# W1's rows of one four-layer residual kernel: moved by on-chip transfers and turned on VectorE instead of TensorE

## Chip, cores and metric

One core of one Trainium2 chip. The metric is the device time of one execution in microseconds, lower is better.

## The reference

`x` has 8 batches of 256 rows and 1024 columns in fp32. Four layers follow each other, each `x = x + f(x)`, with weights of 1024 x 1024:

```python
x = x + (x @ W0.T + (x @ A0[lab0]) @ B0.T * 0.5)
x = x + x @ w_eff.T        # w_eff from W1, see below
x = x + (x @ W2.T + (x @ A2[lab2]) @ B2.T * 0.5)
x = x + (x @ W3.T + 2 * mixture of 8 experts, the two best of each row)
```

The second layer's weight is made from W1 with a change of low rank and a codebook of 8 levels, with one scale per group of 128 columns:

```python
lora_delta = lora_B @ lora_A * 0.5              # rank 64
normalized = (W1 + lora_delta) / scale
quantized = cb[searchsorted(thresholds, normalized)]
w_eff = quantized * scale + lora_delta
```

So `lora_delta` is added twice: before the quantising (the first of the two additions) and after it.

## The kernel before, in words

The layers are linear up to the experts, so the kernel first multiplies the weights with each other (each with the identity added, for the residual) and only then works on `x`. fp32 operands are split into a high and a low part (`_hi` by a cast on ScalarE, `_lo` by a subtraction on VectorE), and each product is three matmuls on TensorE.

The stretch that matters here runs from about 30 to 237 us of the span. TensorE runs passes 1 to 16 (`one_pass`, L1718 for their matmuls). Passes 1 to 8 multiply W2's column blocks with the turned W3 (stage 0; pass 7 is a small one for B2), passes 9 to 16 multiply the blocks of W1 with the result of that and W0 (stage 1). A pass goes over eight tiles k. In stage 1 the right side of tile k is W0's row block k with B0's columns, loaded into `w0_raw`, and the left side is one block of W1, turned, split into `w_hi` and `w_lo` (two buffers each).

W1 comes in eight row blocks of 128 rows, called n or x. For each:

1. SyncE loads it into `a_t` (L456).
2. TensorE multiplies the low-rank factors (`delta`, L1815), and ScalarE copies the result to `ldelta` (`copy_delta`, L732; two buffers).
3. VectorE adds `ldelta` (`add_delta`, L1255), GpSimd adds the identity into `ldelta` (`eye_delta`, L581), ScalarE scales each group (`normalise`, L739).
4. VectorE quantises in three parts (`quantise`, L1241 to L1246: seven thresholds, each but the first a TENSOR_SCALAR into `qtmp` and an addition into `q`), and adds `ldelta` again (L1250), which raises `w1e_done`.
5. TensorE turns the eight tiles of 128 x 128 into PSUM (`turn_w1`, L1706 with `ident,a_t`), in the middle of a pass.
6. ScalarE casts them to `w_hi` (`w1_high`, L690), VectorE subtracts to `w_lo` (`w1_low`, L1131).

Every engine executes its own list in the order written by hand in the kernel, and waits at semaphores. In VectorE's list the parts of `quantise` stand between the low parts of W2 (`w2_low`), W1 and W0 (`w0_low`, L1270). GpSimd's list in this stretch has the identity for W2 (`eye_w2`, L560), for `ldelta`, and for W0 (`eye_w0`, L586). SyncE issues all transfers: after the loads of W1 and W2 come A2's (L501), then, for k from 0 to 7, W0's and B0's row block k (L504, L505), each when TensorE has used tile k of pass 8 (`wait_used`), since `w0_raw` lies where the old low parts lay. W0's row block k then goes through GpSimd (identity), ScalarE (high part, L774) and VectorE (low part) to tile k of pass 9.

`x` is already loaded and turned later in the same way as the change does with W1: four transfers place quarters of it (L510), and VectorE turns blocks of 32 x 32 (`turn_block`, L1424), two instructions of 128 x 512 for 128 rows.

Of the kernel before, what the change touches and what calls it, by code (L numbers as in the profile page):

```python
# [53 lines left out]
def build(nc, x, lab0, codebook, lab2, lab7, W0, A0, B0, W1, scale_log, A1, B1, W2, A2, B2, W3, Wr, A3, B3, out):  # L54
# [19 lines left out]
    Q = 32  # L74
    QUARTERS = P // Q

# [76 lines left out]
    with ExitStack() as ctx:  # L153
# [46 lines left out]
        a2_raw = place("a2_raw", 154368, [P, KT, LABELS * R])  # L200
# [158 lines left out]
        n_ready = sem("n_ready")  # L359
        w1e_done = sem("w1e_done")  # L360
        w1_t = sem("w1_t")
# [87 lines left out]
        def _(sp):  # L449
# [108 lines left out]
        def _(pool):  # L558
# [19 lines left out]
            def eye_delta(n):  # L578
                pool.wait_ge(v_ready, n + 1)
                at = ldelta[n % 2][:, n * P:(n + 1) * P]  # L580
                pool.tensor_tensor(at, at, ident[:], ALU.add).then_inc(ld_eye, 1)  # L581

            def eye_w0(k):
                pool.wait_ge(w0_in[k], 32)
                at = w0_raw[:, k, k * P:(k + 1) * P]
                pool.tensor_tensor(at, at, ident[:], ALU.add).then_inc(w0_eye, 1)  # L586
# [98 lines left out]
        def _(act):  # L685
# [134 lines left out]
            w1_high(4)  # L820
            out_a(3)
            normalise(7)
# [302 lines left out]
        def _(dve):  # L1125
# [110 lines left out]
            def quantise(x, part, steps_=None):  # L1236

                n = a_t[:, x, 0:D].rearrange("p (k i) -> p k i", k=KT)
                if part == 0:
                    dve.wait_ge(n_ready, G1 * (x + 1))  # L1240
                    link(dve.tensor_scalar(q[:], n, th(0), steps[:, 0:1], ALU.is_gt, ALU.mult))  # L1241
# [3 lines left out]
                if part == 2:  # L1245
                    link(dve.scalar_tensor_tensor(out=n, in0=q[:], scalar=book[:, 0:1],  # L1246
                                                  in1=scale[:, x, :].unsqueeze(2).to_broadcast([P, KT, P]),
                                                  op0=ALU.add, op1=ALU.mult))
# [3 lines left out]
            def add_delta(x):  # L1252
                dve.wait_ge(w1_in[x], 16)
# [888 lines left out]
```

## Time and profile before

| | us |
|---|---|
| median of 3 runs | 594.22 |
| lowest, highest run | 594.18, 594.86 |
| span of the profiled execution | 592.8 |
| TensorE busy in it | 585.1 |
| VectorE busy | 447.3 |
| ScalarE busy | 236.4 |
| GpSimd busy | 111.9 |

The span is that of one profiled execution, from its first to its last instruction; the runs' times are device times of other executions and lie 1.4 us above it. Windows and start times below count from the span's start. Engines are named as the profile has them: PE is TensorE, PEld its weight load, DVE VectorE, ACT ScalarE, POOL GpSimd, SP SyncE (SPq its queue of issues). Some names of tiles are shortened by the profile: `w_raw` is `w0_raw`, `a_raw` is `a2_raw` or `a0_raw`.

### The profile page before, as it was taken

The numbers are of one execution on the slowest core, as the hardware profiler recorded it, in microseconds if no ns is written. First come the engines' busy times: TensorE is split into PE (matmuls) and PEld (weight loads), VectorE is DVE, ScalarE is ACT, GpSimd is POOL, SyncE is SP. The second block draws the span as 40 slices with busy tenths as digits, with TensorE's granted clock in tenths as the row PEclk, the third lists the DMA queues.
The fourth block names the chain that finished last, engine by engine and source line by source line (L and its number), as shares of the span: only waits on it lengthen the run. The fifth ranks groups of instructions, "written<-read, shape, count | busy, mean of one in ns | idle before, by whom it ended". The sixth has DMA issues, their size and how long they took to land.

```text
span 592.8 us, 9183 instructions
## 1 busy us (share of the span) xinstructions
PE 585.1 (99%) x3152; PEld 522.2 (88%) x3152; DVE 447.3 (75%) x812; ACT 236.4 (40%) x482; POOL 111.9 (19%) x131
## 2 busy tenths in 40 slices
PE   7999999999999999999999999999999999999998
PEld 6999999899999999999787887787888888888887
DVE  4678998999989855897788999947474747474744
ACT  4534233445432216544465477323333333333331
POOL 3101010012000000336324011041212121212110
PEclk9999999999999999999999999999999999999999
DMA  8962230173000000000243000223031303131301
GB/s 258 231 173 79 87 110 2 26 187 125 1 2 1 1 0 2 2 0 2 25 87 77 1 1 1 65 79 105 37 101 41 107 34 102 40 94 48 107 1 71
DMA packets 56994, 37.19 MB, mean 63 GB/s; under 512 B 25924, under 2 KB 50756, under 8 KB 56964
## 3 DMA queue, kind: packets, MB, share of 16 engines
q1 hardware_dynamic: 56964, 36.79, 22.2%
q8 instruction: 19, 0.31, 0.2%
q14 instruction: 11, 0.09, 0.1%
HBM read 28.39 MB, written 8.39 MB: 62 GB/s over the span
## 4 chain that ended last, share of the span: by engine, by line
PE 73%; DVE 22%; issue 2%; ACT 1%; SPq 1%; DMA 1%; POOL 0%; DVEq 0%; ACTq 0%
PE acc L1864 39%; PE acc L1718 16%; DVE q L1244 6%; PE aux L1864 5%; DVE qtmp L1243 4%; PE acc L1985 4%; PE aux L1706 2%; PE acc L1987 2%; DVE hg_lo L1270 1%; PE acc L1993 1%; PE acc L1994 1%; DVE w_lo L1131 1%; DVE a_t L1255 1%; DMA g<-in_L_cond_W_dram 1%; DVE a_t L1246 1%
## 5 line engine op out<-in xcount | busy, mean ns | idle before, releaser
L1864 PE MATMUL acc<-b_hi,g_lo 128*128 128x512 f32 (+1 forms) x266 | 88.9, 389 | 0.1
L1864 PE MATMUL acc<-t_hi,g_lo 128*128 128x512 f32 x256 | 87.6, 400 | 0.0
L1718 PE MATMUL acc<-hg_hi,w_hi 128*128 128x352 f32 (+1 forms) x376 | 85.3, 334 | 1.6 <-DVE hg_lo L1270 0.8
L1718 PE MATMUL acc<-hg_lo,w_hi 128*128 128x352 f32 (+1 forms) x376 | 84.3, 331 | 0.0
L1718 PE MATMUL acc<-hg_hi,w_lo 128*128 128x352 f32 (+1 forms) x376 | 84.0, 330 | 0.0
L624 POOL TENSOR_TENSOR xr<-xr 128x512 f32<-128x512 f32 x32 | 41.1, 1308 | 144.3 <-DVE g_lo L1435 142.9
L1718 PEld LDWEIGHTS acc<-hg_hi,w_hi 128*128 128x128 f32 x376 | 65.1, 188 | 3.0 <-DVE hg_lo L1270 1.1
L1718 PEld LDWEIGHTS acc<-hg_hi,w_lo 128*128 128x128 f32 x376 | 65.8, 188 | 0.0
L1718 PEld LDWEIGHTS acc<-hg_lo,w_hi 128*128 128x128 f32 x376 | 65.8, 188 | 0.0
L1244 DVE TENSOR_TENSOR q<-q,qtmp 128x1024 f32<-128x1024 f32 x48 | 59.7, 1243 | 1.7
L1864 PEld LDWEIGHTS acc<-b_hi,g_lo 128*128 128x128 f32 x266 | 49.6, 188 | 11.2 <-DVE part L1606 0.5
L1864 PEld LDWEIGHTS acc<-t_hi,g_lo 128*128 128x128 f32 x256 | 48.1, 188 | 11.9 <-DVE c_lo L1610 0.3
L1435 DVE TENSOR_TENSOR g_lo<-xr,g_lo 128x512 fp32r<-128x512 f32 x64 | 43.9, 695 | 15.7 <-ACT g_lo L916 14.4
L916 ACT CAST g_lo<-xr 128x512 fp32r<-128x512 f32 x64 | 39.5, 621 | 39.5 <-DVE xr L1424 29.8
L1864 PE MATMUL acc<-c_lo,g_lo 128*128 128x512 f32 (+1 forms) x132 | 51.2, 388 | 0.0
L640 POOL TENSOR_TENSOR a_t<-a_t 128x512 f32<-128x512 f32 x20 | 28.9, 1464 | 87.8 <-DVE ring_lo L1338 87.5
L1243 DVE TENSOR_SCALAR qtmp<-a_t,thr,steps 128x1024 f32<-128x1024 f32 x48 | 39.2, 817 | 1.3
L1338 DVE TENSOR_TENSOR ring_lo<-a_t,ring_hi 128x512 fp32r<-128x512 f32 x36 | 27.7, 782 | 16.2 <-ACT ring_hi L838 15.9
L1985 PE MATMUL acc<-e_all,g_lo 128*128 128x400 f32 x128 | 38.8, 367 | 0.0
L838 ACT CAST ring_hi<-a_t 128x512 fp32r<-128x512 f32 x36 | 22.3, 622 | 32.0 <-PE acc L1864 17.1
L1987 PE MATMUL acc<-e_all,g_lo 128*128 128x200 f32 x128 | 32.6, 255 | 0.0
L581 POOL TENSOR_TENSOR ldelta<-ldelta,ident 128x128 f32<-128x128 f32 x8 | 6.3, 788 | 120.5 <-DVE a_t L1255 120.5
(301 smaller groups left out, 1140.2 us busy)
## 6 DMA issues: line engine op xcount, KB each, us to landing
out_dram<-part SPq DMA_DIRECT2D x31, 256.0 KB, 2.8
x_st<-in_x_dram SPq DMA_DIRECT2D x60, 128.0 KB, 2.9
g<-in_L_cond_W_dram SPq DMA_DIRECT2D x8, 512.0 KB, 6.3
a_t<-in_L_cond_weight_dram SPq DMA_DIRECT2D x8, 512.0 KB, 5.6
w_raw<-in_L_cond_weight_dram SPq DMA_DIRECT2D x8, 512.0 KB, 4.0
w_st<-in_L_cond_W_dram SPq DMA_DIRECT2D x7, 512.0 KB, 4.0
a_raw<-in_L_cond_lora_A_dram SPq DMA_DIRECT2D x5, 128.0 KB, 3.5
a_raw<-in_L_cond_lora_A_dram SPq DMA_DIRECT2D x20, 32.0 KB, 1.9
```

The costliest lines, as they stand in the source:

```text
L624: pool.tensor_tensor(RAW[dst], RAW[a], RAW[b], op).then_inc(l_sum, 1)
L640: pool.tensor_tensor(c_raw(dst, p), c_raw(a, p), c_raw(b, p), op).then_inc(c_sum, 1)
L838: act.copy(quartered(c_left(name, p)[0]), c_raw(name, p)).then_inc(c_hd, 1)
L916: act.copy(left_hi[:, SLOT[name]], RAW[name]).then_inc(l_hd, 1)
L1243: link(dve.tensor_scalar(qtmp[:], n, th(j), steps[:, j:j + 1], ALU.is_gt, ALU.mult))
L1244: link(dve.tensor_tensor(q[:], q[:], qtmp[:], ALU.add))
L1338: dve.tensor_tensor(quartered(lo), c_raw(name, p), quartered(hi).bitcast(F32), ALU.subtract).then_inc(c_split, 1)
L1435: dve.tensor_tensor(left_lo[:, SLOT[name]], RAW[name], left_hi[:, SLOT[name]].bitcast(F32), ALU.subtract).then_inc(l_split, 1)
L1718: last = pe.matmul(acc[0:a.shape[-1], slot, bank * BANK:bank * BANK + c1 - c0], a[:, k, :], b[:, k, c0:c1], start=(at == 0 and n == 0), st ...
L1864: last = pe.matmul(dst, p, q, start=start and n == 0, stop=stop and n == 2, skip_group_check=True)
L1985: pe.matmul(E_BANK[h], left_hi[:, slot, k % HALF, :], e_all[:, k, :], start=k == 0, stop=False, skip_group_check=True)
L1987: last = pe.matmul(E_BANK[h][:, 0:E_W], left_lo[:, slot, k % HALF, :], e_all[:, k, 0:E_W], start=False, stop=False, skip_group_check=True)
```

## The change

- W1's row block n, after its second addition, is copied within SBUF by 16 transfers of 32 rows by 256 columns from `a_t` to `wq` (`quarter_w1` on SyncE), so that VectorE's 32 x 32 turns (`turn_w1`, two instructions of 128 x 512) give the full turn in `wt`. `wq` and `wt` lie where W2's two staging buffers `w_st` lay. TensorE's `turn_w1` goes; `w1_high` and `w1_low` read `wt` instead of PSUM.
- To match the order of the turned rows, W0 and B0 are loaded in four transfers of 32 rows each instead of one of 128, and the identity goes to the matching places.
- The first of the two additions goes from VectorE to GpSimd (`add_delta`), which then adds the identity as before.
- A2's loads go to another place and stand behind the last `delta`, and the order of several lists is changed.

```diff
         w_st = place("w_st", 154368, [P, 2, KT, P])
-        a2_raw = place("a2_raw", 154368, [P, KT, LABELS * R])
+        wq, wt = place("wq", 154368, [P, D]), place("wt", 158464, [P, KT, P])
+        a2_raw = place("a2_raw", 121600, [P, KT, LABELS * R])
...
-            sp.wait_ge(w_split, splits(KT - 1))
+            def quarter_w1(n):
+                if n == 0:
+                    sp.wait_ge(w_split, splits(KT - 2))
+                else:
+                    sp.wait_ge(w1_t, 2 * n)
+                sp.wait_ge(w1e_done, n + 1)
+                for c in range(QUARTERS):
+                    for a in range(QUARTERS):
+                        sp.dma_start(wq[a * Q:(a + 1) * Q, c * QD:(c + 1) * QD],
+                                     row(n, slice(c * Q, (c + 1) * Q))[:, a * QD:(a + 1) * QD]).then_inc(wq_in, 16)
+
+            quarter_w1(0)
+            quarter_w1(1)
+            for k in range(KT):
+                wait_used(sp, KT, k)
+                for a in range(QUARTERS):
+                    rows = slice((a * KT + k) * Q, (a * KT + k + 1) * Q)
+                    sp.dma_start(w0_raw[a * Q:(a + 1) * Q, k, 0:D], W0[rows, :]).then_inc(w0_in[k], 16)
+                    sp.dma_start(w0_raw[a * Q:(a + 1) * Q, k, D:C_A], B0[rows, :]).then_inc(w0_in[k], 16)
+            for n in range(2, KT - 1):
+                quarter_w1(n)
+            sp.wait_ge(ld_done, KT)
             for l in range(LABELS):
                 sp.dma_start(a2_raw[:, :, l * R:(l + 1) * R], A2[l].rearrange("(k p) r -> p k r", p=P)).then_inc(a2_in, 16)
-            for k in range(KT):
-                wait_used(sp, KT, k)
-                sp.dma_start(w0_raw[:, k, 0:D], W0[k * P:(k + 1) * P, :]).then_inc(w0_in[k], 16)
-                sp.dma_start(w0_raw[:, k, D:C_A], B0[k * P:(k + 1) * P, :]).then_inc(w0_in[k], 16)
+            quarter_w1(KT - 1)
...
-            def eye_delta(n):
+            def add_delta(n):
+                pool.wait_ge(w1_in[n], 16)
+                pool.wait_ge(ld_ready, n + 1)
+                pool.tensor_tensor(row(n), row(n), ldelta[n % 2][:], ALU.add).then_inc(v_ready, 1)
                 pool.wait_ge(v_ready, n + 1)
                 at = ldelta[n % 2][:, n * P:(n + 1) * P]
                 pool.tensor_tensor(at, at, ident[:], ALU.add).then_inc(ld_eye, 1)
...
             eye_w2(1)
-            for n in range(4):
-                eye_w2(n + 2)
-                eye_delta(n)
+            eye_w2(2)
+            add_delta(0)
+            eye_w2(3)
+            add_delta(1)
+            eye_w2(4)
+            eye_w2(5)
+            add_delta(2)
             eye_w2(6)
+            add_delta(3)
             eye_w2(7)
-            eye_delta(4)
+            add_delta(4)
+            add_delta(5)
             for k in range(KT):
                 eye_w0(k)
-            for n in (5, 6, 7):
-                eye_delta(n)
+            add_delta(6)
+            add_delta(7)
...
             def w1_high(n):
-                act.wait_ge(w1_t, n + 1)
+                act.wait_ge(w1_t, 2 * (n + 1))
                 act.wait_ge(acc_done, pass_of(KT + n - 2) + 1)
-                w_high(n, aux[:, :].rearrange("p (k o) -> p k o", k=KT))
+                w_high(n, wt[:])
...
-            def add_delta(x):
-                dve.wait_ge(w1_in[x], 16)
-                dve.wait_ge(ld_ready, x + 1)
-                dve.tensor_tensor(row(x), row(x), ldelta[x % 2][:], ALU.add).then_inc(v_ready, 1)
+            def turn_w1(n):
+
+                dve.wait_ge(w_split, splits(KT + n - 1))
+                dve.wait_ge(wq_in, 16 * QUARTERS * QUARTERS * (n + 1))
+                for half in range(2):
+                    ks = slice(half * HALF, (half + 1) * HALF)
+                    dve.transpose(wt[:].rearrange("p k (c r) -> p c k r", r=Q)[:, :, ks].bitcast(U32),
+                                  wq[:].rearrange("p (c k q) -> p c k q", c=QUARTERS, q=Q)[:, :, ks].bitcast(U32)
+                                  ).then_inc(w1_t, 1)
...
+            w2_low(7)
             quantise(3, 1)
-            w2_low(7)
-            add_delta(4)
             quantise(3, 2)
+            turn_w1(0)
             quantise(4, 0)
...
             w1_low(0)
+            turn_w1(1)
             w0_low(0)
             w0_low(1)
...
             w1_low(1)
-            add_delta(5)
             quantise(4, 2)
+            turn_w1(2)
             quantise(5, 0)
             w1_low(2)
             quantise(5, 1)
-            add_delta(6)
+            turn_w1(3)
+            quantise(5, 2)
             w1_low(3)
-            quantise(5, 2)
             quantise(6, 0)
+            turn_w1(4)
             quantise(6, 1)
             w1_low(4)
-            add_delta(7)
             quantise(6, 2)
-            quantise(7, 0, (1,))
+            turn_w1(5)
+            quantise(7, 0)
             w1_low(5)
-            quantise(7, 1, (2, 3, 4))
+            quantise(7, 1)
+            turn_w1(6)
+            quantise(7, 2)
             w1_low(6)
-            quantise(7, 2)
+            turn_w1(7)
             w1_low(7)
...
-            DELTA_AT = {(1, 3): 0, (1, 6): 1, (10, 0): 6, (12, 0): 7}
+            DELTA_AT = {(1, 3): 0, (1, 6): 1, (10, 0): 6, (11, 0): 7}
             B1_AT = (1, 0)
-            TURN_W1_AT = {p: (5 if p in (KT + 2, KT + 4) else 3) for p in range(KT, 2 * KT)}
...
-                    if TURN_W1_AT.get(p) == k:
-                        turn_w1(p - KT)
-
```

## Rows read from the trace of the kernel before

**Rows 1.** The page, part 1: busy time, share and instructions of each engine.
```profile
PE 585.1 (99%) x3152; PEld 522.2 (88%) x3152; DVE 447.3 (75%) x812; ACT 236.4 (40%) x482; POOL 111.9 (19%) x131
```

**Rows 2.** Waits of TensorE, 30 to 240 us: in total, times, longest.
```profile
PE acc L1718 <- DVE hg_lo L1270: 0.8, 1, 0.8
```

**Rows 3.** The chain that ended last, 100 to 240 us: start, length, what.
```profile
142.40 6.08 PE acc L1718 x36
...
204.51 0.87 PE aux L1706 x8
...
217.88 18.84 PE acc L1718 x117
```

**Rows 4.** Timeline of VectorE: start, length, what; the idle time before it.
```profile
104.87 0.81 DVE L1241 TENSOR_SCALAR q<-a_t,thr,steps 128x1024 f32<-128x1024 f32 x1
...
115.29 1.22 DVE L1255 TENSOR_TENSOR a_t<-a_t,ldelta 128x1024 f32<-128x1024 f32 x1
116.42 0.81 DVE L1243 TENSOR_SCALAR qtmp<-a_t,thr,steps 128x1024 f32<-128x1024 f32 x1
...
123.24 0.81 DVE L1241 TENSOR_SCALAR q<-a_t,thr,steps 128x1024 f32<-128x1024 f32 x1
...
148.04 0.80 DVE L1243 TENSOR_SCALAR qtmp<-a_t,thr,steps 128x1024 f32<-128x1024 f32 x1
...
154.85 0.81 DVE L1241 TENSOR_SCALAR q<-a_t,thr,steps 128x1024 f32<-128x1024 f32 x1
```

**Rows 5.** Timeline of VectorE, instructions with idle time before them.
```profile
46.50 0.81 DVE L1241 TENSOR_SCALAR q<-a_t,thr,steps 128x1024 f32<-128x1024 f32 x1 [2.19 <-ACT a_t L739]
...
97.06 1.22 DVE L1131 TENSOR_TENSOR w_lo<-w_st,w_hi 128x1024 fp32r<-128x1024 f32 x1 [2.13 <-ACT w_hi L690]
```

**Rows 6.** GpSimd's lines (min/median/max ns), and both engines' timelines at two places.
```profile
L640 POOL TENSOR_TENSOR a_t<-a_t x20: 1283/1320/1819, 241.1 to 303.7; 128x512 f32<-128x512 f32 x20
...
L560 POOL TENSOR_TENSOR w_st<-w_st,ident x8: 455/458/1440, 5.0 to 95.8; 128x128 f32<-128x128 f32 x8
...
252.14 5.17 POOL L640 TENSOR_TENSOR a_t<-a_t 128x512 f32<-128x512 f32 x4 [5.17 <-DVE ring_lo L1338]
...
252.17 1.29 DVE L1219 TENSOR_SCALAR labf<-labf 1x16 f32<-1x16 f32 x1
...
295.39 1.67 POOL L640 TENSOR_TENSOR a_t<-a_t 128x512 f32<-128x512 f32 x1 [5.44 <-DVE ring_lo L1338]
...
295.23 0.69 DVE L1358 TENSOR_TENSOR g_lo<-g,cb_hi 128x512 fp32r<-128x512 f32 x1
295.83 1.78 DVE L1358 TENSOR_TENSOR ct_lo<-ct,ct_hi 128x512 fp32r<-128x512 f32 x1
```

**Rows 7.** VectorE's turns of x: min/median/max ns.
```profile
L1424 DVE STREAM_TRANSPOSE xr<-x_st x30: 666/686/714, 313.1 to 558.4; 128x512 uint32<-128x512 uint32 x30
```

**Rows 8.** SyncE's issues: lines with min/median/max ns, and five in a row.
```profile
L504 SPq DMA_DIRECT2D w_raw<-in_L_cond_weight_dram x8: 328/328/340, 123.0 to 135.0; - x8
...
L505 SPq DMA_DIRECT2D w_raw<-in_L_cond_lora_B_w_dram x8: 432/432/722, 123.4 to 135.3; - x8
...
L510 SPq DMA_DIRECT2D x_st<-in_x_dram x60: 311/317/449, 307.2 to 554.6; - x60
...
310.73 2.42 SPq L528 DMA_DIRECT2D a_raw<-in_L_cond_lora_A_dram  x5
```

**Rows 9.** The page, part 6: transfers, KB each, median us to landing.
```profile
x_st<-in_x_dram SPq DMA_DIRECT2D x60, 128.0 KB, 2.9
...
a_raw<-in_L_cond_lora_A_dram SPq DMA_DIRECT2D x20, 32.0 KB, 1.9
```

**Rows 10.** W0's high part by line (busy, mean ns), low part (min/median/max ns).
```profile
L774 ACT CAST hg_hi<-w_raw 128x1056 fp32r<-128x1056 f32 x8 | 8.6, 1080 | 4.8 <-POOL w_raw L586 4.8
...
L1270 DVE TENSOR_TENSOR hg_lo<-w_raw,hg_hi x8: 1243/1324/1521, 131.1 to 144.6; 128x1056 fp32r<-128x1056 f32 x8
```

**Rows 11.** TensorE's first turns: min/median/max ns.
```profile
L1706 PE MATMUL acc<-ident x19: 272/421/475, 1.6 to 6.5; 128*128 128x128 f32 x19
```

More of the change, by code:

```diff
@@ L74, in build @@
     Q = 32
+    QD = D // 4
     QUARTERS = P // Q
@@ L359, in build @@
         n_ready = sem("n_ready")
+        dq_ready = sem("dq_ready")
         w1e_done = sem("w1e_done")
+        wq_in = sem("wq_in")
         w1_t = sem("w1_t")
@@ L583, in eye_w0 @@
             def eye_w0(k):
-                pool.wait_ge(w0_in[k], 32)
-                at = w0_raw[:, k, k * P:(k + 1) * P]
-                pool.tensor_tensor(at, at, ident[:], ALU.add).then_inc(w0_eye, 1)
+                pool.wait_ge(w0_in[k], 16 * 2 * QUARTERS)
+                at = w0_raw[:, k, 0:D].rearrange("p (a k q) -> p a k q", a=QUARTERS, q=Q)[:, :, k]
+                pool.tensor_tensor(at, at, ident[:].rearrange("p (a q) -> p a q", a=QUARTERS), ALU.add).then_inc(w0_eye, 1)
             for k in range(KT):
@@ L820, in _ @@
             w1_high(4)
+            normalise(7)
             out_a(3)
-            normalise(7)
             w1_high(5)
@@ L1240, in quantise @@
                     dve.wait_ge(n_ready, G1 * (x + 1))
+                    if x:
+                        dve.wait_ge(dq_ready, x)
                     link(dve.tensor_scalar(q[:], n, th(0), steps[:, 0:1], ALU.is_gt, ALU.mult))
@@ L1245, in quantise @@
                 if part == 2:
-                    link(dve.scalar_tensor_tensor(out=n, in0=q[:], scalar=book[:, 0:1],
-                                                  in1=scale[:, x, :].unsqueeze(2).to_broadcast([P, KT, P]),
-                                                  op0=ALU.add, op1=ALU.mult))
+                    dve.scalar_tensor_tensor(out=n, in0=q[:], scalar=book[:, 0:1],
+                                             in1=scale[:, x, :].unsqueeze(2).to_broadcast([P, KT, P]),
+                                             op0=ALU.add, op1=ALU.mult).then_inc(dq_ready, 1)
+                    dve.wait_ge(dq_ready, x + 1)
                     dve.wait_ge(ld_eye, x + 1)
                     dve.tensor_tensor(row(x), row(x), ldelta[x % 2][:], ALU.add).then_inc(w1e_done, 1)
-            def add_delta(x):
-                dve.wait_ge(w1_in[x], 16)
-                dve.wait_ge(ld_ready, x + 1)
-                dve.tensor_tensor(row(x), row(x), ldelta[x % 2][:], ALU.add).then_inc(v_ready, 1)
+            def turn_w1(n):
[6 more added lines that the diff above has]
+                                  ).then_inc(w1_t, 1)
             def add_bp(rows, slot, psum_rows, width):
@@ L1265, in w1_low @@
             def w1_low(n):
-                w_low(n, aux[:, :].rearrange("p (k o) -> p k o", k=KT), KT + n + 1)
+                w_low(n, wt[:], KT + n + 1)
             def w0_low(k):
@@ L1273, in _ @@
             w2_low(2)
-            add_delta(0)
             split_b2()
@@ L1278, in _ @@
             w2_low(3)
-            add_delta(1)
             quantise(0, 2)
@@ L1283, in _ @@
             quantise(1, 1)
-            add_delta(2)
             quantise(1, 2)
@@ L1288, in _ @@
             quantise(2, 1)
-            add_delta(3)
             w2_low(6)
@@ L1807, in delta @@
                     pe.wait_ge(a1_hd, 2)
-                elif n < 6:
+                else:
                     pe.wait_ge(ld_ready, n)
-                else:
-                    pe.wait_ge(w_split, splits(KT + 2 * n - 11))
                 for a, first in ((a_hi, True), (a_lo, False)):
@@ L1817, in delta @@
                 last.then_inc(ld_done, 1)
-            def turn_w1(n):
-                pe.wait_ge(w1e_done, n + 1)
-                if n in (0, 2, 4):
-                    pe.wait_ge(ld_ready, 6 + n // 2)
-                else:
-                    pe.wait_ge(w_split, splits(KT + n - 1))
-                for k in range(KT):
-                    last = turn_tile(aux[:, k * P:(k + 1) * P], a_t[:, n, k * P:(k + 1) * P])
-                last.then_inc(w1_t, 1)
             DELTA_FIRST = {3: 2, 4: 3, 5: 4, 7: 5}
-            DELTA_AT = {(1, 3): 0, (1, 6): 1, (10, 0): 6, (12, 0): 7}
+            DELTA_AT = {(1, 3): 0, (1, 6): 1, (10, 0): 6, (11, 0): 7}
             B1_AT = (1, 0)
-            TURN_W1_AT = {p: (5 if p in (KT + 2, KT + 4) else 3) for p in range(KT, 2 * KT)}
             def one_pass(stage, p, t):
```

## The prediction

> **What bounds the kernel now.** The page's first part says that TensorE is busy for 99% of the span [rows 1]. A busy figure alone can hide waits, so the next view is who waited for whom on that engine from 30 to 240 us, the stretch in which the change lies: one wait, 0.8 us, for VectorE's low part of a W0 tile [rows 2]. The chain of waits says the same in order of time: from 142.40 us to the end of the stretch every piece is TensorE's own, and W1's turns stand in it as pieces of 0.87 us for eight tiles [rows 3]. So TensorE's work is the time here, and work taken off it is worth its whole length, provided that what replaces it is ready in time. How near the others are to being late is the second question. VectorE stands in the chain until 142.40 us (the only wait is for it), and it works almost without a gap from 104.87 to 154.85 us [rows 4]. It is the engine with no room, and the change gives it more to do.
>
> The profiled execution has a span of 592.8 us; the median of the runs is 594.22 us. I count differences on the span and add them to the median. A change of 0.2% (1.2 us) is about what can be told from none.
>
> **TensorE's side.** Eight turns of 0.87 us leave it [rows 3]: 8 x 0.87 = 7.0 us, all on the path before. The change of low rank for row block 7 moves from one pass to another and costs the same.
>
> **VectorE up to the first turn.** Row block 3 takes VectorE from 104.87 to 123.24 us [rows 4]: 18.4 us with one addition (the next instruction starts 1.13 later, 115.29 to 116.42) and one low part of W2 (of the addition's length [rows 5], so 1.1) in it, so about 16.0 us of quantising a row block. In the new order the thresholds of row block 4 are reached after:
> - minus four additions (row blocks 1 to 4), 4 x 1.13 = 4.5 us. The addition of row block 0 frees nothing: VectorE sat idle for ScalarE's scaling there [rows 5], and that scaling also waits for VectorE's table of exponentials;
> - minus the idle 2.1 us before the low part at 97.06 us [rows 5]. It came from GpSimd's identity for W2, which stood behind VectorE's addition of row block 3 and now stands ahead of it;
> - plus what the additions on GpSimd take from VectorE. A GpSimd addition of 128 columns takes 0.46 us, one of 512 takes 1.28 us at least [rows 6], so one of 1024 takes 1.28 + 0.82 x 512/384 = 2.4 us. The same rows show what stands beside it: during four GpSimd additions in a row a VectorE instruction on 16 elements took 1.29 us, and a subtraction that takes 0.69 us took 1.78 us beside one of them: 1.1 us lost to 1.28 us of GpSimd [rows 6]. For the whole of a 2.4 us addition that is 2.2 us; four of them 8.8 us. The one of row block 0 holds back that table instead, for about as long as the scaling waited for VectorE's addition before: nothing.
>
> 123.24 - 4.5 - 2.1 + 8.8 = 125.4 us. Then come the two halves of the first turn. VectorE's turns of 128 x 512 take 0.69 us each [rows 7], with the wait 1.3 us: the first is done at 126.7 us.
>
> What I extrapolate is that VectorE is held for the whole addition; the rows show it only for instructions of 1.3 us. If the lock were given back in between, each would cost the 1.1 us of the row and the six on the path 6.6 us less (612.4 us instead of 619). The Trainium skill, SBUF — State Buffer, Who interferes with whom, says that the shared port pair is taken for the full instruction and the other engine is blocked fully, also by a tensor_tensor with two inputs in SBUF; by that rule it is the 2.2 us.
>
> **SyncE's queue.** This is the largest term. SyncE now issues 16 small transfers for W1's row block 1 before it issues any of W0's, and it may do so only when the first turn is done. Issues cost it time whatever their size: 0.33 us for 512 KB, 0.43 us for 16 KB, 0.31 us at the least for 32 rows [rows 8], and the next starts 0.04 to 0.05 us later (five in 2.42 us are 0.49 us apart). No transfer within the chip is in the trace; I take 0.37 us an issue, W0's pitch, since it has the same plain form, with 0.35 and 0.49 as ends. 16 x 0.37 = 5.9: row block 1 is out at 132.6 us. W0 and B0 went out in 16 issues, 0.8 of every 1.7 us, at the pace at which TensorE freed the rows (123.0 to 135.0 us). Now they are 64 issues: 4 x (0.37 + 0.48) = 3.4 us a tile, 8 x 3.4 = 27.2 us. The last leaves at 159.9 us instead of 135.8. It lands 2.9 us later, as x did with 128 KB on 32 rows (1.9 us for 32 KB is the other end) [rows 9], then 0.46 us of GpSimd, 1.08 of ScalarE and 1.3 of VectorE [rows 6, 10]: 165.8 us with the hops. TensorE, which needs 1.6 us for a tile, gets one every 3.4 us, and ends that pass at 167.3 us instead of 148.5: 18.8 us lost. VectorE idles too, for its work is in order and W0's low parts stand in front of the rest of row block 4.
>
> **VectorE after it.** What is left from 165.8 us to the end of row block 7: a low part of W1 (1.1), the rest of row block 4 (6.8, from 148.04 to 154.85) [rows 4], three row blocks (3 x 16.0 = 48.0), four low parts (4.6), five turns (6.5), and two GpSimd additions in the way (4.4; that of row block 5 falls where VectorE waits). Together 71.4: 237.2 us. The low part of row block 6 then lets TensorE start the last pass but one at 238.3 us; free since some 227 us, it has waited. It runs two passes (the last 13 tiles before took 18.84 us, so 11.6 each): 261.5 us. The tail of row block 7 just fits beside the first of them: 16 issues 5.9, landing 1.9 [rows 9], turn 1.3, ScalarE 1.1, VectorE 1.1 and hops end at 248.8, and TensorE asks for it at 249.9. Before, the stage ended at 236.7 us [rows 3]. Behind it nothing is changed.
>
> Sum: 261.5 - 236.7 = 24.8 us longer, the 7.0 us of turns already taken off. Span 617.6 us, time 619.0 us.
>
> **The rivals.**
> - *GpSimd's additions cost nothing* (they fall into gaps). Against it are the two stretched instructions [rows 6] and VectorE's lack of gaps. Then 8.8 and 4.4 us of the sum go, the stage ends at 261.5 - 13.2 = 248.3, and it is 11.6 us longer: 605.8 us. The queue alone costs that.
> - *The queue is no limit.* If an issue cost next to nothing, W0 would come at TensorE's pace, VectorE would be done with it at 152.6 us (126.7, two of three parts of row block 4 at 16.0 - 6.8 = 9.2, the sum for B2 1.5, W1's low part 1.1, a turn 1.3, eight low parts 10.6, one blocked addition 2.2), and 71.4 + 1.1 + 23.2 us later the stage ends at 248.3: 11.6 us longer, 605.8 us. The Trainium skill, DMA: Bandwidth & Descriptors, Anatomy of one DMA, gives about 50 ns for a dispatch, on GpSimd's path, and calls the descriptors' cost small; SyncE's rows show 0.31 us and more.
> - *Faster.* Both at once: GpSimd's additions hold nobody and issues hide behind the pace of the rows. Then VectorE is through W0 at 144 us, as before, TensorE waits for nothing and keeps its 7.0 us: 587.2 us. It decides at 0.2 us an issue (eight in 1.6 us); the least in the trace is 0.31 us [rows 8], so almost everything speaks against it.
> - *Slower still.* All issues at 0.49 us add 1.9 + 4.2, and TensorE after its waits may run slowly, as in its first instructions, where a turn takes 0.42 us against 0.27 [rows 11]; on the two last passes perhaps 2 us each (an estimate: a dozen such turns and what follows). Together 629 us.
>
> **How the numbers follow.** Forecast with both mechanisms, 612 to 627 us: 0.65. One of them missing, 603 to 612: 0.20. Beyond 627, by the slow end: 0.08. Faster: 0.05. No change, a cancelling: 0.02. Faster 0.05, same 0.02, slower 0.93. The range of 8 in 10 takes the forecast's own, the two rivals at 606 and a part of the slow end: 603 to 629 us.
>
> **What would show it.** In the changed profile: W0's and B0's issues from about 133 to 160 us, back to back, 64 of them at 0.33 to 0.43 us; TensorE waiting for VectorE's low parts of W0, each some 2 us, in sum near 20; GpSimd's additions at 2.4 us or more, and beside each a VectorE instruction of 3 us instead of 0.8 or 1.2; quantising of row block 7 done near 237 us; waits of TensorE for W1's low parts. VectorE's turns at 0.69 us. The prediction is wrong if W0's issues keep TensorE's pace, if VectorE's instructions beside GpSimd's additions keep their lengths, or if TensorE's waits there stay under 7 us.

## The result, and the profile after

Median 629.85 us over four runs (628.6 to 630.1), before 594.2: 35.6 us longer, a ratio of 1.060 (95% interval 1.058 to 1.061). Forecast were 619.0 us, in a range of 603 to 629. The direction and the order of the stations were as forecast; the size was not.

The profiled execution has a span of 628.4 us, 35.6 more than before. The page's first part (busy us, share of the span, instructions):

```profile
PE 587.4 (93%) x3088; PEld 521.0 (83%) x3088; DVE 463.8 (74%) x820; ACT 236.8 (38%) x482; POOL 134.7 (21%) x139
```

TensorE was busy for 99% of the span [rows 1], now for 93%. Its idle time went from 7.7 to 41.0 us, so nearly all of the 35.6 us went into waiting. Its busy time is 2.3 us longer although 64 turns (7.0 us) are gone: three passes take 13.3 or 13.4 us instead of 11.8 (see the clock below), and pass 9, the one that uses W0, takes 15.1 us without its waits, where it took 12.0 us without its waits and its turns. Who is waited for on TensorE from 30 to 275 us (in total, times, longest):

```profile
PE acc L1758 <- DVE hg_lo L1310: 22.9, 8, 10.4
PE acc L1758 <- DVE w_lo L1163: 8.2, 5, 2.8
PE aux L1853 <- DVE w_lo L1163: 3.1, 1, 3.1
```

Before, this view had one wait of 0.8 us [rows 2]. Now 34.2 us are spent on it: two thirds for the low parts of W0 (`hg_lo`), the rest for those of W1. VectorE is named each time, but it is only the last hand. The chain of waits, the same stretch as [rows 3], tells who kept it:

```profile
124.58 1.31 DVE wt L1293 x2
125.91 0.51 SPq L512
...
128.36 1.46 SPq L512
...
136.83 0.58 SPq L521
...
166.53 2.18 DMA w_raw<-in_L_cond_lora_B_w_dram
...
170.37 1.26 DVE hg_lo L1310
171.62 1.14 DVE w_lo L1163
...
223.73 0.51 SPq L512
...
233.15 1.84 DMA wq<-a_t
235.11 1.30 DVE wt L1293 x2
...
243.13 0.52 SPq L512
...
253.25 1.88 DMA wq<-a_t
255.22 1.32 DVE wt L1293 x2
...
257.64 1.24 DVE w_lo L1163
258.92 13.31 PE acc L1758 x72
```

Where TensorE stood from 142.40 us on [rows 3], there are now three stretches: SyncE's issues (L512 is `quarter_w1`, L521 and L522 are W0 and B0) from 125.9 to 166.5 us; VectorE's own work from 170.4 to 243.1, but for one piece from 223.7 to 235.1 us in which the chain goes over row block 6's issues and their landing (VectorE has other work beside them and idles only the last 1.1 us); and a tail of issues, landing, turn, high and low part from 243.1 to 258.9, for which the last pass waited. The stage ends at 272.2 us, where it ended at 236.7.

The timeline of SyncE's queue (start, length of the issues):

```profile
98.82 37.97 SPq L512 DMA_DIRECT2D wq<-a_t  x32
136.83 0.58 SPq L521 DMA_DIRECT2D w_raw<-in_L_cond_weight_dram  x1
...
142.85 0.42 SPq L521 DMA_DIRECT2D w_raw<-in_L_cond_weight_dram  x1
143.32 0.42 SPq L522 DMA_DIRECT2D w_raw<-in_L_cond_lora_B_w_dram  x1
...
166.53 0.42 SPq L522 DMA_DIRECT2D w_raw<-in_L_cond_lora_B_w_dram  x1
```

Row blocks 0 and 1 are 32 issues; the second sixteen start at 125.91, when the first turn is done, and are out at 136.83. Then W0 and B0 go out one behind the other, 0.46 us apart, 30 us long. Before, 16 issues left between 123.0 and 135.3 us, with pauses. The one line of the on-chip transfers, L512 (shortest, median and longest in ns), and what the queue had already shown before for W1's eight loads of 512 KB (kernel before, L456):

```profile
L512 SPq DMA_DIRECT2D wq<-a_t x128: 507/591/1595, 98.8 to 253.3; - x128
```

```profile
L456 SPq DMA_DIRECT2D a_t<-in_L_cond_weight_dram x8: 328/579/3122, 23.5 to 85.0; - x8
```

An on-chip issue takes 0.59 us, and the next begins 0.04 later. The forecast had 0.37 for both together and 0.49 as the upper end. The row of L456 was in the trace before and would have put that end at 0.58 us at least.

VectorE beside GpSimd's addition (the timeline of VectorE, then that of GpSimd):

```profile
107.07 3.31 DVE L1278 TENSOR_TENSOR q<-q,qtmp 128x1024 f32<-128x1024 f32 x1
...
111.29 1.22 DVE L1278 TENSOR_TENSOR q<-q,qtmp 128x1024 f32<-128x1024 f32 x1
```

```profile
106.71 2.59 POOL L604 TENSOR_TENSOR a_t<-a_t,ldelta 128x1024 f32<-128x1024 f32 x1 [15.21 <-ACT ldelta L764]
```

The addition from 106.71 to 109.30 us ends inside one VectorE addition of 3.31 us, whose like takes 1.22: 2.1 us lost. Seven of the eight additions have such a partner: four VectorE additions of 3.3 us and three thresholds of 2.8 instead of 0.8. The eighth, row block 0's, holds one of the small instructions of the table of exponentials, where nobody waits.

Station by station, from the chain and the timelines:

| | forecast | measured |
|---|---|---|
| first turn done | 126.7 | 125.9 |
| row block 1 issued | 132.6 | 136.8 |
| W0 and B0 issued | 159.9 | 167.0 |
| last low part of W0 | 165.8 | 171.6 |
| row block 7 quantised | 237.2 | 243.1 |
| last low part of W1 | 248.8 | 258.9 |
| stage ends | 261.5 | 272.2 |

### The profile page after: what moved, and what is told of

It is laid out like the page before. It is cut to its first block, busy times and chain, and to the rows that moved or that the text cites. A ratio compares the mean times of both kernels' runs of the same rounds, so it can differ in the third digit from the quotient of the medians.

```text
span 628.4 us, 9262 instructions
## 1 busy us (share of the span) xinstructions
PE 587.4 (93%) x3088; PEld 521.0 (83%) x3088; DVE 463.8 (74%) x820; ACT 236.8 (38%) x482; POOL 134.7 (21%) x139
## 4 chain that ended last, share of the span: by engine, by line
PE 56%; DVE 28%; SPq 8%; issue 3%; DMA 2%; ACT 1%; POOL 0%; DVEq 0%; ACTq 0%
PE acc L1888 37%; DVE q L1278 9%; DVE qtmp L1277 6%; PE aux L1888 5%; SPq L512 5%; PE acc L1758 4%; PE acc L2009 4%; DVE w_lo L1163 2%; PE acc L2011 2%; DVE a_t L1280 2%; SPq L521 2%; SPq L522 1%; DVE wt L1293 1%; PE acc L2017 1%; PE acc L2018 1%
## 5 line engine op out<-in xcount | busy, mean ns | idle before, releaser
L1758 PE MATMUL acc<-hg_hi,w_hi 128*128 128x352 f32 (+1 forms) x376 | 88.6, 344 | 32.0 <-DVE hg_lo L1310 22.9
L1758 PEld LDWEIGHTS acc<-hg_hi,w_hi 128*128 128x128 f32 x376 | 67.0, 194 | 37.4 <-DVE hg_lo L1310 14.7
L1758 PE MATMUL acc<-hg_lo,w_hi 128*128 128x352 f32 (+1 forms) x376 | 86.3, 338 | 0.0
L1758 PE MATMUL acc<-hg_hi,w_lo 128*128 128x352 f32 (+1 forms) x376 | 85.8, 336 | 0.0
L1278 DVE TENSOR_TENSOR q<-q,qtmp 128x1024 f32<-128x1024 f32 x48 | 67.9, 1416 | 1.7
L1758 PEld LDWEIGHTS acc<-hg_lo,w_hi 128*128 128x128 f32 x376 | 67.8, 193 | 0.0
L1758 PEld LDWEIGHTS acc<-hg_hi,w_lo 128*128 128x128 f32 x376 | 67.6, 193 | 0.0
L1888 PEld LDWEIGHTS acc<-t_hi,g_lo 128*128 128x128 f32 x256 | 48.1, 188 | 11.9 <-DVE c_lo L1650 0.3
L948 ACT CAST g_lo<-xr 128x512 fp32r<-128x512 f32 x64 | 39.5, 621 | 38.6 <-DVE xr L1464 28.4
L1277 DVE TENSOR_SCALAR qtmp<-a_t,thr,steps 128x1024 f32<-128x1024 f32 x48 | 45.0, 938 | 1.3
L604 POOL TENSOR_TENSOR a_t<-a_t,ldelta 128x1024 f32<-128x1024 f32 x8 | 22.0, 2748 | 81.5 <-ACT ldelta L764 81.5
L1378 DVE TENSOR_TENSOR ring_lo<-a_t,ring_hi 128x512 fp32r<-128x512 f32 x36 | 25.6, 725 | 9.8 <-ACT ring_hi L870 9.6
```

The costliest lines, as they stand in the source:

```text
L948: act.copy(left_hi[:, SLOT[name]], RAW[name]).then_inc(l_hd, 1)
L1277: link(dve.tensor_scalar(qtmp[:], n, th(j), steps[:, j:j + 1], ALU.is_gt, ALU.mult))
L1278: link(dve.tensor_tensor(q[:], q[:], qtmp[:], ALU.add))
L1378: dve.tensor_tensor(quartered(lo), c_raw(name, p), quartered(hi).bitcast(F32), ALU.subtract).then_inc(c_split, 1)
L1758: last = pe.matmul(acc[0:a.shape[-1], slot, bank * BANK:bank * BANK + c1 - c0], a[:, k, :], b[:, k, c0:c1], start=(at == 0 and n == 0), st ...
L1888: last = pe.matmul(dst, p, q, start=start and n == 0, stop=stop and n == 2, skip_group_check=True)
```

## The experiments

**My theory:** SyncE's list of issues holds back W0 and with it VectorE, which then needs its full time to the end; GpSimd's additions hold VectorE; a dear on-chip issue lengthens head and tail. **The rivals:** the additions cost nothing, or nearly all; the queue is no limit and VectorE's added work alone makes the time; the order of W0's wait in the queue, not the number of issues, is the trouble; the last pass is slow by TensorE's clock.

### The additions: back to VectorE, and alone

The first kernel is the change with `add_delta` on VectorE again and GpSimd with the identity alone, the second the kernel before with only this part of the change.

```diff
-            def add_delta(n):
-                pool.wait_ge(w1_in[n], 16)
-                pool.wait_ge(ld_ready, n + 1)
-                pool.tensor_tensor(row(n), row(n), ldelta[n % 2][:], ALU.add).then_inc(v_ready, 1)
+            def eye_delta(n):
                 pool.wait_ge(v_ready, n + 1)
...
+            def add_delta(x):
+                dve.wait_ge(w1_in[x], 16)
+                dve.wait_ge(ld_ready, x + 1)
+                dve.tensor_tensor(row(x), row(x), ldelta[x % 2][:], ALU.add).then_inc(v_ready, 1)
```

> The changed kernel with the first addition back on VectorE (and GpSimd's list as before the change); W1 still moved by transfers and turned on VectorE. Theory 1, SyncE's queue sets the end (16 issues of 0.63 us a row block, 64 issues of 0.47 us for W0): VectorE gets back 4 x 2.1 us by the first turn, pays 4 x 1.13 and perhaps the idle 2.1 us, so the first turn moves by 2 to 4 us and the time falls by 3 to 6 us, to 624 to 627 us. Theory 2, the blocked port is the main cost: the time falls by half of the 35.6 us or more, to 612 us or less.

> The kernel before with only the first addition moved to GpSimd (GpSimd's list as in the change); TensorE turns W1, W0 comes whole. Theory 1: VectorE is later by about 1 us for each addition (2.1 less 1.13), TensorE had a few us of slack at W1's turns and 0.8 us of waits at W0, GpSimd's addition of row block 5 now stands ahead of W0's identity: 595 to 599 us. Theory 2: most of the loss is here, 606 us or more.

Measured: 627.86 us (ratio 1.056, 1.055 to 1.058) without the additions on GpSimd, and 599.76 us (1.010, 1.008 to 1.011) with them alone. TensorE's waits from 30 to 275 us, first kernel:

```profile
PE acc L1762 <- DVE hg_lo L1306: 17.7, 7, 10.1
PE acc L1762 <- DVE w_lo L1154: 7.5, 3, 3.5
PE aux L1857 <- DVE w_lo L1154: 2.2, 1, 2.2
```

and second:

```profile
PE acc L1714 <- DVE w_lo L1140: 2.8, 4, 1.2
PE acc L1714 <- DVE hg_lo L1274: 2.3, 2, 1.5
```

So the additions on GpSimd are a loss by themselves, 5.7 us: each frees 1.1 us of VectorE and takes 2.1. In the whole change they are worth 2.0 us only (629.85 - 627.86), for the first turn comes just 1.5 us earlier without them (124.4 us) and the queue behind it is as long as ever. The two do not add: 5.7 alone, 33.8 for everything else, 35.6 together.

### The queue: W0 whole, and W1 in four transfers

In the first of these W0 and B0 are loaded in one transfer each, as before; the order of columns that this needs is made by the quarters of W1, in pieces of 32 columns. The bytes and the number of W1's transfers are the same.

```diff
-                        sp.dma_start(wq[a * Q:(a + 1) * Q, c * QD:(c + 1) * QD],
-                                     row(n, slice(c * Q, (c + 1) * Q))[:, a * QD:(a + 1) * QD]).then_inc(wq_in, 16)
+                        sp.dma_start(wq[a * Q:(a + 1) * Q, c * QD:(c + 1) * QD].rearrange("p (k q) -> p k q", q=Q),
+                                     row(n, slice(c * Q, (c + 1) * Q)).rearrange("p (k a q) -> p a k q", a=QUARTERS,
+                                                                                 q=Q)[:, a]).then_inc(wq_in, 16)
...
-                for a in range(QUARTERS):
-                    rows = slice((a * KT + k) * Q, (a * KT + k + 1) * Q)
-                    sp.dma_start(w0_raw[a * Q:(a + 1) * Q, k, 0:D], W0[rows, :]).then_inc(w0_in[k], 16)
-                    sp.dma_start(w0_raw[a * Q:(a + 1) * Q, k, D:C_A], B0[rows, :]).then_inc(w0_in[k], 16)
+                sp.dma_start(w0_raw[:, k, 0:D], W0[k * P:(k + 1) * P, :]).then_inc(w0_in[k], 16)
+                sp.dma_start(w0_raw[:, k, D:C_A], B0[k * P:(k + 1) * P, :]).then_inc(w0_in[k], 16)
```

> The changed kernel with W0 and B0 loaded in one transfer each per tile, as before; W1's quarters take every fourth run of 32 columns instead, so that the order of the sum matches. 128 transfers for W1 stay, now in pieces of 128 bytes. Theory 1: 48 issues of 0.47 us go, W0 is out by about 144 us instead of 167, VectorE becomes the bound of that pass near 153 us instead of 171.6: the time falls by some 18 us, to 609 to 614 us, if an issue of small pieces still costs 0.6 us. Theory 2: under 8 us gained. If pieces of 128 bytes make an on-chip issue dearer than 0.8 us, the gain is lost again.

The other leaves W0 as in the change and moves W1's row block in four transfers of 32 x 1024. The exchange of quarters is left out, so the second layer's product is another one; the work of the engines stays.

```diff
                 for c in range(QUARTERS):
-                    for a in range(QUARTERS):
-                        sp.dma_start(wq[a * Q:(a + 1) * Q, c * QD:(c + 1) * QD],
-                                     row(n, slice(c * Q, (c + 1) * Q))[:, a * QD:(a + 1) * QD]).then_inc(wq_in, 16)
+                    rows = slice(c * Q, (c + 1) * Q)
+                    sp.dma_start(wq[rows], row(n, rows)).then_inc(wq_in, 16)
```

> The changed kernel with each row block of W1 moved by 4 transfers of 32 rows x 1024 columns to the same rows, without the exchange of quarters: the second layer's product is then another one, the work of every other instruction is the same. Theory 1: 12 issues of 0.63 us (7.6 us) go ahead of W0 and 7.6 us in the tail; the tail no longer decides and VectorE does: 35.6 less 10 to 14 us, 615 to 620 us. If the cost lies in bytes and not in issues, the 16 issues' 10.7 us stay and the time stays at 629 us.

Measured: 618.72 us with W0 whole (ratio 1.042, 1.040 to 1.044) and 617.05 us with four transfers (1.039, 1.037 to 1.040), that is 11.1 and 12.8 us less than the change. The first came out above its 609 to 614 us, though an issue kept its price: the last low part of W0 is done at 159.0 us (171.6 in the change), not near 153. In its chain of waits a tile of W0 lands only 4.2 us after its issue, and two pieces of quantising row block 4 stand between W0's low parts on VectorE; what each of the two costs, no run shows. The on-chip issues of the two, W0 whole first:

```profile
L512 SPq DMA_DIRECT2D wq<-a_t x128: 585/611/1577, 98.7 to 242.1; - x128
```

```profile
L512 SPq DMA_DIRECT2D wq<-a_t x32: 507/592/598, 99.0 to 236.5; - x32
```

A transfer with four times the bytes is issued in the same 0.59 us: an issue is paid by the piece. Both rivals that leave the queue out fall here, since these edits change neither VectorE's nor GpSimd's work. The tail shows the price too: with W0 whole it is 247.9 - 231.8 = 16.1 us, with four transfers 242.6 - 234.6 = 8.0 (end of row block 7 to the last low part of W1).

Then all three together: additions on VectorE, W0 whole, four transfers.

> Three things of the change undone at once: the first addition back on VectorE, W0 and B0 in one transfer each, W1's row blocks in 4 transfers of 32 x 1024 without the exchange of quarters (so the second layer's product is another one). What stays is VectorE's turning. Theory 1 (issues are the cost): VectorE ends row block 7 about 4 us later than before the change (eight turns of 1.3 us less its idle time), the tail of 2.4 + 2.4 + 1.3 + 1.05 + 1.1 us ends near 227 us, and with TensorE's 7.0 us saved the time is 594 to 599 us. If something else in the change costs (the turns' place, the order of the lists), it stays above 603 us.

601.49 us (1.011, 1.010 to 1.013), above the 594 to 599 I expected. TensorE's waits:

```profile
PE acc L1759 <- DVE w_lo L1151: 5.0, 2, 3.5
PE acc L1759 <- DVE hg_lo L1303: 4.1, 4, 1.8
PE aux L1854 <- DVE w_lo L1151: 1.4, 1, 1.4
```

The stage ends at 245.7 us, 9.0 later than before: 10.5 us of waits (0.8 before), 7.0 us of turns less, and 6.3 us in which TensorE works slower behind the waits (pass 14, behind the longest, takes 14.5 us instead of 11.8; see the clock below). These are figures of the profiled execution, which took 603.58 us, 2.1 above the median. From 150 to 208 us the chain of waits runs over VectorE, whose turns, thresholds and low parts follow each other in it, and no longer over the queue. So 28.4 of the 35.6 us are the queue's and the additions' together (629.85 - 601.49), and with them gone there are still 7.1 us of loss. By the chain I put them down to VectorE's added work in the order it is given; no run of the whole change tells its amount from its order.

### What makes an on-chip issue dear

The same 16 transfers to the same places, from W1's rows in DRAM instead of `a_t`. The turned block is then W1 itself and not the quantised weight, so the second layer has another weight; all waits stay.

```diff
-                                     row(n, slice(c * Q, (c + 1) * Q))[:, a * QD:(a + 1) * QD]).then_inc(wq_in, 16)
+                                     W1[n * P + c * Q:n * P + (c + 1) * Q, a * QD:(a + 1) * QD]).then_inc(wq_in, 16)
```

> The changed kernel with the 16 transfers a row block taken from W1 in DRAM instead of from SBUF, in the same shape (32 rows x 256 columns), so that the second layer's weight is the plain one. If an issue is dear because its source lies on the chip, an issue takes 0.33 to 0.42 us here instead of 0.59, row block 1 goes out 3 to 4 us sooner, the tail is as much shorter, and the time falls by 6 to 8 us, to 622 to 624 us. If it is dear for its shape or for its place in the list, it stays at 0.59 us and 630 us.

```profile
L512 SPq DMA_DIRECT2D wq<-in_L_cond_weight_dram x128: 310/421/1602, 99.2 to 247.3; - x128
```

622.50 us (1.048, 1.046 to 1.049), 7.4 less than the change. With the source in DRAM the median issue falls from 591 to 421 ns, which is that of W0's loads in the change; shape, number and destination are the same, so the source makes this difference. It is not all that sets a price: issues of 512 KB from DRAM took 0.33 us behind an idle queue (W0 before [rows 8]) and 0.58 right behind a load of W2 (three of L456's eight), and W0's first load in the change took 0.58 right behind an on-chip transfer (136.83 us). Why, no run shows.

### The order of the queue

W0 is not put behind row block 1 any more: of its sixteen issues six stand between W0's loads and ten behind them, and VectorE's second turn stands behind W0's low parts. With W0 whole and the additions on VectorE.

```diff
             quarter_w1(0)
-            quarter_w1(1)
             for k in range(KT):
...
+                if k == 1:
+                    sp.wait_ge(w1_t, 2)
+                    sp.wait_ge(w1e_done, 2)
+                if k >= 1:
+                    quarter(1, k - 1)
+            for at in range(KT - 1, QUARTERS * QUARTERS):
+                quarter(1, at)
```

> The whole change with its costs moved: additions on VectorE, W0 and B0 in one transfer each (W1's quarters take runs of 32 columns), and the 16 transfers of row block 1 stand between and behind W0's loads instead of ahead of them. Theory 1: W0 keeps TensorE's pace, the pass of W0 loses under 5 us; only the tail behind row block 7 is left (10.9 of issues, 2.0 landing, 3.5 for turn, high and low part): stage end near 248 us, 603 to 608 us.

610.67 us (1.027, 1.026 to 1.029), 19.2 less than the change, and above my 603 to 608. W0 now flows: its issues run from 123.2 to 137.2 us and pass 9 from 134.1 to 149.7. But the load moved to the next station: `wq` has one buffer, so row block 2 can be issued only when the second turn is done (148.3 us), its turn is done at 162.5, and TensorE waits for W1 instead:

```profile
PE acc L1770 <- DVE w_lo L1162: 8.1, 3, 3.5
PE aux L1865 <- DVE w_lo L1162: 6.3, 2, 5.3
PE acc L1770 <- DVE hg_lo L1314: 3.3, 2, 1.8
```

The tail is as long as in the change, 240.2 - 224.0 = 16.2 us. W0 whole gave 11.1 us and the additions 2.0; the other 6 of the 19.2 us are the order's (a difference of three runs, for the costs do not add exactly). So the order explains a part of the loss ahead of W0, and none of the tail.

### The clock in the last pass

The last pass takes 13.3 us in the change and took 11.8 before. In the experiment, 32 turns of the identity fill TensorE's wait ahead of it.

```diff
             def one_pass(stage, p, t):
+                if p == 2 * KT:
+                    pe.wait_ge(ld_ready, KT)
+                    for _ in range(32):
+                        turn_tile(aux[:, 0:P], ident[:])
```

> The changed kernel with 32 more turns of the identity on TensorE ahead of its last pass (into PSUM that nobody reads), where it waited 2.8 us. The clock theory: the last pass, 13.3 us after that wait against 11.7 us where none stands ahead, takes 11.7 us again and the time falls by 1.6 us, to 628.2 us; if the turns last longer than the wait, a part of it is lost. If the length of that pass has another cause, it stays at 13.3 us.

Windows of the change first (length, then busy time and instructions of PE, PEld, DVE, ACT and POOL, granted clock, DMA share, GB/s), then of the experiment:

```profile
244.00:256.00 12.00, 11.75 (x72) 11.57 (x72) 0.97 (x3) 0.39 (x1) 0.00 (x0) 1.00 0.17 45
258.00:260.00 2.00, 1.08 (x4) 1.08 (x5) 1.55 (x2) 1.06 (x2) 0.00 (x0) 0.69 0.00 0
260.00:265.00 5.00, 5.00 (x27) 5.00 (x27) 2.06 (x4) 2.29 (x4) 0.00 (x0) 0.78 0.01 2
265.00:272.00 7.00, 7.00 (x45) 7.00 (x45) 5.31 (x16) 5.23 (x19) 0.00 (x0) 1.00 0.00 0
```

```profile
255.00:259.00 4.00, 4.00 (x38) 3.98 (x36) 2.64 (x4) 2.52 (x3) 0.00 (x0) 1.00 0.00 0
259.00:271.00 12.00, 12.00 (x76) 11.95 (x75) 8.06 (x23) 7.84 (x24) 0.00 (x0) 1.00 0.01 2
```

TensorE had waited 2.8 us, and came back at a granted clock of 0.69 and 0.78, a mixture of its two levels, 2.4 and 1.2 GHz; from 265 us it had the full one. So the slow pass and the lower granted clock go together. With the wait filled it has the full one throughout, and the pass takes 11.6 us (from 259.18 to 270.75 in the chain). That the filling did it is not shown, for pass 15 of the same execution began behind a wait with nothing in it and had the full clock too. The wait is the only one of that execution from 230 us on, and ends at 243.8:

```profile
PE acc L1758 <- DVE w_lo L1163: 3.4, 1, 3.4
```

```profile
245.00:250.00 5.00, 5.00 (x33) 5.00 (x32) 0.00 (x0) 0.00 (x0) 0.00 (x0) 1.00 0.18 49
```

That pass took 11.9 us. So a wait of this length does not always bring the slow clock, and what decides stays open. That the filling shortens the run is not shown either: the median is 630.64 us over runs from 628.39 to 632.42, beside 629.85 for the change, and the span is 1.7 us shorter. In the change itself the two other passes that begin behind a wait of 2.2 us or more are as slow, 13.3 and 13.4 us, and those behind a wait of about 1 us or none take 11.7 to 11.9. In other kernels it goes both ways: with four transfers pass 14 took 11.8 us behind 2.2 us, with W0 whole pass 13 took 13.4 us behind 1.9 us.

### Is there a share of it that pays?

The kernel before, with row blocks 2 and 3 alone taken off TensorE: their transfers stand behind all of W0's loads, which stay whole (the quarters in pieces of 32 columns again), and VectorE turns them right after W1's low parts of row blocks 1 and 2. The additions stay on VectorE. A further kernel adds row block 4.

```diff
+    SOME = (2, 3)
...
             def w1_low(n):
-                w_low(n, aux[:, :].rearrange("p (k o) -> p k o", k=KT), KT + n + 1)
+                w_low(n, wt[:] if n in SOME else aux[:, :].rearrange("p (k o) -> p k o", k=KT), KT + n + 1)
+                if n + 1 in SOME:
+                    turn_dve(n + 1)
...
-                    if TURN_W1_AT.get(p) == k:
+                    if TURN_W1_AT.get(p) == k and p - KT not in SOME:
                         turn_w1(p - KT)
```

> The kernel before with only row blocks 2 and 3 moved by transfers and turned on VectorE, behind W0's loads in SyncE's list; the others are turned on TensorE, all additions are on VectorE. TensorE saves 2 x 0.87 us, VectorE pays 2 x 1.3 us out of its slack of about 5 us ahead of the last pass, SyncE is idle there. 592.5 us, 1.7 us less than before; if VectorE's slack is used up otherwise, the same time.

> As the run before, with row blocks 2, 3 and 4. TensorE saves 2.6 us, VectorE pays 3.9 us and is then about as late as TensorE is early: 591.6 to 594 us. If VectorE is the bound by then, more than with two row blocks.

Both missed: 597.08 us (1.004, 1.003 to 1.006) with two row blocks, 605.18 us (1.018, 1.016 to 1.019) with three. TensorE's waits, two row blocks and then three:

```profile
PE acc L1747 <- DVE w_lo L1149: 2.3, 1, 2.3
PE acc L1747 <- DVE hg_lo L1299: 0.8, 1, 0.8
```

```profile
PE acc L1747 <- DVE w_lo L1149: 9.3, 2, 6.6
```

With two, one wait of 2.3 us ahead of pass 11 and its slow pass (13.4 us instead of 11.8) cost 3.9 us, against the 1.7 us of the turns. Next I moved only what that wait was for: W1's low part of row block 2 ahead of a part of quantising, the turns placed by themselves, ScalarE's high part before a copy.

```diff
             w1_low(1)
+            turn_dve(2)
             add_delta(5)
             quantise(4, 2)
-            quantise(5, 0)
             w1_low(2)
+            quantise(5, 0)
+            turn_dve(3)
             quantise(5, 1)
```

> As the kernel with row blocks 2 and 3 turned on VectorE, which lost 2.3 us at one wait of TensorE for W1's low part of row block 2 (and 1.6 us in the pass behind it). Here that low part stands ahead of row block 5's thresholds on VectorE, ScalarE makes the high part ahead of copying the low-rank product, and the second turn comes behind the first thresholds. If lateness at that one place was the whole loss, TensorE waits as before the change only, 2 x 0.87 us are saved: 592.5 us. If VectorE's sum of work decides, 595 us or more.

596.83 us (1.004, 1.003 to 1.005): the wait of 2.3 us only moved, from 160.8 to 185.8 us, to W1's low part of row block 4. I read that as VectorE's sum at work. The last run tests that reading: the low parts of row blocks 4 and 5 are moved in the same way, and nothing else.

```diff
             quantise(6, 0)
-            quantise(6, 1)
             w1_low(4)
+            quantise(6, 1)
             add_delta(7)
             quantise(6, 2)
-            quantise(7, 0, (1,))
             w1_low(5)
+            quantise(7, 0, (1,))
```

> The kernel of the run before with W1's low parts of row blocks 4 and 5 also moved ahead in VectorE's list (that of row block 4 ahead of the second part of quantising row block 6, that of row block 5 ahead of the first part of row block 7). VectorE's total and SyncE's list stay. If the 2.3 us wait at 185.8 us is only a matter of place, TensorE has no wait over 0.5 us and keeps the 1.7 us of its two turns less: 592.6 us. If VectorE's sum decides, the wait turns up once more, at a later pass of W1 (from 198 us on), TensorE runs slowly behind it, and the time stays at 595 us or more.

592.46 us over eleven runs, beside 593.74 for the kernel before over fifteen: ratio 0.9975 (0.9966 to 0.9984). The reading fell: it was place. TensorE's waits, and the chain to the end of the stage:

```profile
PE acc L1747 <- DVE hg_lo L1297: 0.8, 1, 0.8
```

```profile
181.23 0.87 PE aux L1735 x8
...
216.65 18.84 PE acc L1747 x117
235.48 4.37 PE acc L1893 x24
```

TensorE has the one wait it had before [rows 2] and no other, its turns (0.87 us, L1735) leave out row blocks 2 and 3 and go on with row block 4 at 181.23 us, and the stage ends at 235.5 us, 1.2 earlier. This is the one kernel of the study that beats the kernel before, by 0.25%. It moves two of eight row blocks, leaves W0's loads and the additions as they were, and puts the transfers where the queue is empty.

## Why the prediction was right, and where it was wrong

- **TensorE's 7.0 us** did come off; no matmul of the stage turns W1 any more. But they were not "all on the path before": two of the eight turns, at 126.0 and 139.1 us, stand ahead of the wait that ends at 142.40 us, where the chain of the kernel before runs over VectorE, so six of them (5.2 us) were worth their length. Only the rival "faster" uses this figure. The 7.0 us were bought with 34.2 us of waits, as forecast in kind (waits of nearly 20 us for W0's low parts forecast, 22.9 measured).
- **GpSimd's additions holding VectorE** came as forecast. 2.2 us were forecast for VectorE, 2.1 measured beside each addition; the extrapolation from instructions of 1.3 us stood. With it stood the rule of the Trainium skill, SBUF — State Buffer, Who interferes with whom, that the other engine is blocked for the full instruction. The rival "the additions cost nothing" (605.8 us) falls by the kernel with them alone. What the sum did not say is that this loss hides behind the queue in the whole change: 2.0 us there, 5.7 alone.
- **The step that failed** is in SyncE's queue: "No transfer within the chip is in the trace; I take 0.37 us an issue, W0's pitch, since it has the same plain form, with 0.35 and 0.49 as ends." It is 0.63 us, above the upper end, and it stands in the sum twice: ahead of W0 (16 issues in 10.9 us instead of 5.9, one of them 1.46 us) and in the tail (10.7 instead of 5.9). The mechanism was right and its price was mis-sized; it was taken as the same form, and the run with the source in DRAM shows that the source makes 0.17 us of the difference.
- **W0's 64 issues** were 27.2 us in the forecast and 30.1 measured (0.46 us apart instead of 0.42, and a gap of 0.4 behind the first), 2.9 us more. Their landing took 2.2 us instead of 2.9.
- **From there to row block 7** VectorE needs 71.5 us, forecast 71.4. The sum for the engine that sets the rate was right to 1.1 us: so long does VectorE idle in it for row block 6's transfers, which the sum did not have, and its work took as much less.
- **The tail** was forecast to fit beside the last pass but one with 1.1 us to spare. With issues at 0.63 us it takes 15.8 us instead of 11.6 and becomes the wait for the last pass; the slow clock behind that wait adds 1.7 us to the forecast's 11.6. That clock stood in the text as a rival ("on the two last passes perhaps 2 us each"), and was not in the sum.
- **The miss adds up**: 5.9 us later at row block 7, 4.2 in the tail, minus the 1.1 to spare, 1.7 of clock: 10.7 us, from 261.5 to 272.2.
- **The rival "the queue is no limit"** (605.8 us) falls by the two runs that only take issues away, 11.1 and 12.8 us. SyncE's rows show 0.42 us for a load and 0.59 us for an on-chip transfer. The Trainium skill, DMA: Bandwidth & Descriptors, Anatomy of one DMA, gives some 50 ns for a dispatch, on GpSimd's path; no transfer here goes that way.
- **The chances.** The slow end was given 0.08 and needed issues at 0.49 us and two slow passes. The first came and more, of the second about half, so the range should have reached over it. Its own sum was short, too: with issues at 0.49 us the tail takes 1.9 us more and has only 1.1 to spare, which adds 0.8. And a price whose only known relatives run to 0.58 us (L456) had no business ending at 0.49.

Left open: why an SBUF source makes an issue dearer, and whether a second buffer for `wq` or issues from another engine's queue would help; neither was tried.

## What to carry to other kernels

Count the transfers before the bytes: sixteen small on-chip transfers cost their queue 10 us, whatever they carry, and everything issued behind them is late by that. When work moves from the bounding engine to one that is nearly full, move only what fits: two of eight blocks gained 0.25% where all eight lost 6%, and even the two gained only once each low part stood where the next pass asks for it. A wait that wanders to the next consumer after an edit is not yet proof that the engine's sum decides.

## What the runs showed of the hardware that I had not expected

- In a row of its like, a transfer out of SBUF is 0.59 us of SyncE's time to issue, one of the same shape out of DRAM 0.42; 32 KB or 128 KB makes no difference (0.591 and 0.592), and pieces of 128 bytes add 0.02 (0.611). Single issues among them take 1.3 to 1.6 us. What stands ahead matters too: in the kernel with the quarters between, W0's load takes 0.33 us behind an idle queue and mostly 0.60 right behind an on-chip transfer.
- Behind most waits of 2.2 us or more TensorE's granted clock was under 1.0 at first (0.69 and 0.78 in the last pass of the change), and the pass of 11.8 us took 13.3 to 13.4, so 1.6 us on top of the wait; behind one of 3.5 us it took 14.5 (all three parts undone). It is no rule: a wait of 3.4 us (the kernel with 32 turns, pass 15) and one of 2.2 us (four transfers, pass 14) had no slow pass behind them, and one of 1.9 us had (W0 whole, pass 13, granted clock 0.56 over its first 3.7 us).
